# Column sums as adding transfers, and self entries of twelve columns, in a graph-and-experts kernel

## The reference

```
x   (1250, 512), src and dst (40000,): edges, dst sorted
xn  = layernorm(x)
h   = relu(xn @ W1 + b1) @ W2 + b2            # 512 -> 256 -> 512
agg[i] = sum of h[dst[e]] over edges e with src[e] == i
x1  = x + h + agg
xn2 = layernorm(x1)
gate = softmax(xn2 @ W_gate + b_gate); thr = sigmoid(xn2 @ W_thr + b_thr) * 0.25
w    = max(gate - thr, 0), divided by its sum over the 8 experts (1 where it is 0)
out  = x1 + sum over experts e of w[:, e] * (xn2 @ W_exp[e] + b_exp[e])
```

## Time and profile before

| | |
|---|---|
| median of 3 runs | 350.18 us (349.97 to 350.19) |
| the profiled execution | 349.31 us |
| its span, first to last instruction | 347.5 us |
| PE busy | 335.9 us, 97% of the span |
| DVE busy | 295.4 us, 85% |
| ACT busy | 119.4 us, 34% |
| POOL busy | 83.4 us, 24% |
| chain of waits, PE's share | 89%; DVE 5% |
| granted TensorE clock | 0.999 |
| bytes moved | 22.09 MB |

### The profile page before, as it was taken

The page is one execution under the profiler, slowest core; times in us unless marked ns, Lnnn a source line. Parts: engine busy times, 40 slices in busy tenths (PEclk is TensorE's granted clock), DMA queues, the critical chain, the costliest instruction groups (busy, mean ns, idle before and its releaser), DMA issues.

```text
span 347.5 us, 7647 instructions
## 1 busy us (share of the span) xinstructions
PE 335.9 (97%) x2637; PEld 261.4 (75%) x2637; DVE 295.4 (85%) x571; ACT 119.4 (34%) x233; POOL 83.4 (24%) x151
## 2 busy tenths in 40 slices
PE   8699999999999999999999999999999999999995
PEld 7589875665555645576678888888888888888884
DVE  7799999998896889977968888888898888888774
ACT  6898843454542036767213130030030200300000
POOL 5000032434343004429132140400500503200000
PEclk9999999999999999999999999999999999999999
DMA  7955132334443400040000030300300300000133
GB/s 171 253 155 195 49 85 52 80 75 96 88 86 86 136 0 0 2 126 3 0 0 2 6 116 3 116 7 2 123 1 2 121 2 2 1 2 0 61 119 120
DMA packets 20226, 22.09 MB, mean 64 GB/s; under 512 B 11850, under 2 KB 12647, under 8 KB 20188
## 3 DMA queue, kind: packets, MB, share of 16 engines
q1 hardware_dynamic: 17420, 18.36, 19.1%
q0 software_dynamic: 2352, 2.71, 3.4%
q10 hardware_dynamic: 416, 0.53, 0.7%
HBM read 12.77 MB, written 2.56 MB: 44 GB/s over the span
## 4 chain that ended last, share of the span: by engine, by line
PE 89%; DVE 5%; issue 2%; DMA 1%; ACT 1%; DVEq 0%; SPq 0%; ACTq 0%
PE ps_g L1195 13%; PE ps_g L1394 11%; PE ps_g L1396 11%; PE ps_g L1395 11%; PE ps_w L1255 8%; PE ps_g L1183 5%; PE ps_g L1318 3%; PE ps_a L1394 2%; PE ps_a L1396 2%; PE ps_a L1395 2%; PE ps_w L1394 2%; PE ps_w L1396 2%; PE ps_w L1395 2%; PE ps_w L1234 2%; PE ps_g L1360 2%
## 5 line engine op out<-in xcount | busy, mean ns | idle before, releaser
L1067 DVE SCALAR_TENSOR_TENSOR x_sb<-ps_g,weight_s,x_sb 125x256 f32<-125x256 f32 (+1 forms) x142 | 75.1, 547 | 19.5 <-PE ps_g L1396 18.4
L865 DVE TENSOR_TENSOR split<-places,keys 125x756 f16<-125x756 int16 (+4 forms) x119 | 73.2, 676 | 4.0 <-issue 2.2
L1394 PE MATMUL ps_g<-wb_hi,places 128*128 128x256 f16 x212 | 57.8, 273 | 0.1
L1396 PE MATMUL ps_g<-wb_hi,r_sb 128*128 128x256 f16 x212 | 57.8, 273 | 0.0
L1395 PE MATMUL ps_g<-wb_lo,places 128*128 128x256 f16 x212 | 57.8, 273 | 0.0
L1195 PE MATMUL ps_g<-late,r_sb 125*128 125x512 f32 (+3 forms) x120 | 51.5, 533 | 0.3 <-DMA late<-counts 0.2
L401 POOL DMA_DIRECT2D late<-counts x49 | 28.3, 577 | 79.6 <-ACT counts L599 79.0
L1255 PEld LDWEIGHTS ps_w<-split 125*128 125x128 f16 x476 | 29.9, 97 | 14.2 <-issue 6.4
L1396 PE MATMUL ps_g<-wb_hi,split 128*128 128x256 f16 x142 | 38.7, 273 | 0.0
L1394 PE MATMUL ps_g<-wb_hi,split 128*128 128x256 f16 x142 | 38.7, 273 | 0.0
L1395 PE MATMUL ps_g<-wb_lo,split 128*128 128x256 f16 x142 | 38.7, 273 | 0.0
(11 more groups left out here) (232 smaller groups left out, 675.3 us busy)
## 6 DMA issues: line engine op xcount, KB each, us to landing
stage<-in_L_ffn_W_exp_dram SPq DMA_DIRECT2D x8, 1024.0 KB, 5.2
late<-counts SPq DMA_DIRECT2D x54, 58.6 KB
late<-counts POOLq DMA_DIRECT2D x41, 58.6 KB, 2.8
x_sb<-in_x_dram SPq DMA_DIRECT2D x5, 448.0 KB, 11.5
out_dram<-x_sb SPq DMA_DIRECT2D x10, 224.0 KB
w_sb<-in_L_gnn_W_dram SPq DMA_DIRECT2D x2, 512.0 KB, 11.0
out_dram<-x_sb ACTq DMA_DIRECT2D x10, 26.0 KB
b_sb<-in_L_gnn_b_dram SPq DMA_DIRECT2D x1, 250.0 KB
```

The costliest lines, as they stand in the source:

```text
L865: nc.vector.tensor_tensor(hot[hot_at(stage, p)][:, 0:n, :].rearrange("p c (k x j) -> p c k x j", k=SEGS, j=2), places_of(windows[s], n), k ...
L1067: nc.vector.scalar_tensor_tensor(out=x_sb[:, i, a:z], in0=bank[0:R, at:at + z - a], scalar=weight_s[:, expert_of(u), i:i + 1], in1=x_sb[:, ...
L1394: nc.tensor.matmul(out_cols, hi_x, wb_hi[par][:, q, k, :], start=(opens and k == 0), stop=False, skip_group_check=True)
L1396: mm = nc.tensor.matmul(out_cols, lo_x, wb_hi[par][:, q, k, :], start=False, stop=(k == 1), skip_group_check=True)
```

## The change

Three edits.

1. **Column sums.** POOL issues a transfer for each of the tiles 0 to 8: tile 0 is copied to `a_sum`, tiles 1 to 8 are added to it by the transfer itself (`accum_op=ALU.add`), each 125 partitions of 1250 fp32, 625,000 bytes. A transfer waits for the tile's moves and for the sum before it. They stand behind POOL's move of group LAST[i] + 3 (SUM_LAG = 3; 9 for tile 0), and that of tile 8 behind the last group. Moves into a tile buffer wait for the transfer that read it. DVE keeps the last add alone (`last_sum`), behind the transfer of tile 8.
2. **Self entries.** One matmul for each run of rows that lies in one tile: its moving operand is 12 columns or fewer of `self_at` (the identity in fp16), its output the columns where the entries lie; all 128 partitions take part. Two matmuls in most groups, three in the nine border groups, one in the three groups with one window: 114 in place of 63. Two fills on POOL and one of two small ACT casts at the start fall away.
3. **Block sums.** Expert 1's four block sums on DVE move from behind groups 5, 6, 7, 8 to behind groups 28, 29, 31, 32.

```diff
-    SUM_LAG = 7
+    SUM_LAG = 3
...
-        self_lo = sb("self_lo", [128, 3 * LO + 2 * WIN], F16)
+        self_at = sb("self_at", [128, 2 * WIN], F16)
...
-                        eng.wait_ge(a_summed, max(tile - 3, 1))
+                        eng.wait_ge(a_added, 16 * (tile - 2))
...
+            def column_sum(i):
+
+                moved(pool, i)
+                if i > 0:
+                    pool.wait_ge(a_added, 16 * i)
+                if i == 0:
+                    pool.dma_start(a_sum, a_t[0]).then_inc(a_added, 16)
+                else:
+                    pool.dma_start(a_sum, a_t[i % 3], accum_op=ALU.add).then_inc(a_added, 16)
+
             begun = [2]
+            COLUMNS_AT = {max(LAST[i] + SUM_LAG, POOL_MOVES): i for i in range(TILES - 2)}
             for g in range(POOL_MOVES, NG):
                 pool.wait_ge(win_out, g + 1)
                 move(pool, g, 1, begun)
+                if g in COLUMNS_AT:
+                    column_sum(COLUMNS_AT[g])
+            column_sum(TILES - 2)
...
-            act.wait_ge(self_base, 2)
             act.wait_ge(const_ready, CONSTS)
-            for a in (0, WIN):
-                at = LO if a == 0 else 2 * LO + WIN
-                nc.scalar.activation(self_lo[0:2 * WIN, at:at + WIN], ident[0:2 * WIN, a:a + WIN], ACT.Copy).then_inc(self_ready, 1)
+            nc.scalar.activation(self_at[:, :], ident[:, 0:2 * WIN], ACT.Copy).then_inc(self_ready, 1)
...
-            def column_sum(i):
-
-                moved(dve, i)
-                if i > 1:
-                    dve.wait_ge(a_summed, i - 1)
-                nc.vector.tensor_tensor(a_sum, a_t[0] if i == 1 else a_sum, a_t[i % 3], ALU.add).then_inc(a_summed, 1)
+            def last_sum():
+
+                moved(dve, TILES - 1)
+                dve.wait_ge(a_added, 16 * (TILES - 1))
+                nc.vector.tensor_tensor(a_sum, a_sum, a_t[(TILES - 1) % 3], ALU.add).then_inc(a_summed, 1)
...
-            SUM_AT = {5: T1, 6: T3, 7: T2, 8: T4}
-            COLUMNS_AT = {LAST[i] + SUM_LAG: i for i in range(1, TILES - 2)}
+            SUM_AT = {28: T1, 29: T3, 31: T2, 32: T4}
...
-                if g in COLUMNS_AT:
-                    column_sum(COLUMNS_AT[g])
-            column_sum(TILES - 2)
...
-            column_sum(TILES - 1)
+            last_sum()
...
             def self_entries(g, pieces):
 
                 bank = ps_w[g % 2]
...
+                for n, (s, a, z, tile, at) in enumerate(MOVES[g]):
+                    own = nc.tensor.matmul(bank[:, s * LO + at:s * LO + at + z - a], self_pos[:, HI - 1 - tile:HI - 1 - tile + 128],
+                                           self_at[:, s * WIN + a:s * WIN + z], start=(n == 0), stop=False, skip_group_check=True)
+                    if n == 0 and g > 0 and g - 1 not in pieces and (g > SLOTTED or last_step_of(g - 1) % SLOT_STEPS > 0):
+                        own.then_inc(win_done, 1)
...
-            pe.wait_ge(a_summed, TILES - 1)
+            pe.wait_ge(a_summed, 1)
```

More of the change, by code:

```diff
@@ L130, in gnn_moe @@
         ones = sb("ones", [128, 128])
-        zeros = sb("zeros", [1, BANK], F16)
         eps = sb("eps", [128, 1])
@@ L270, in gnn_moe @@
         pool_moved = [sem(f"pool_moved{q}") for q in range(RINGS)]
-        a_summed = sem("a_summed")
+        a_summed, a_added = sem("a_summed"), sem("a_added")
         g_done = sem("g_done")
@@ L504, in _ @@
             group_rows(fill, (row_inv, "inv"), (row_size, "size"), (row_base, "base"))
-            nc.gpsimd.memset(zeros[:, :], 0.0).then_inc(self_ready, 1)
             nc.gpsimd.memset(self_pos[:, :], 0.0).then_inc(self_base, 1)
-            nc.gpsimd.memset(self_lo[:, :], 0.0).then_inc(self_base, 1)
-            pool.wait_ge(self_base, 2)
+            pool.wait_ge(self_base, 1)
             pool.wait_ge(const_ready, CONSTS)
@@ L1227, in self_entries @@
                 bank = ps_w[g % 2]
[L1228 to L1233, removed]
-                own = nc.tensor.matmul(bank[:, 0:cols], self_pos[0:rows, HI - 1 - tile:HI - 1 - tile + 128],
-                                       self_lo[0:rows, LO - at:LO - at + cols], start=True, stop=False, skip_group_check=True)
-                if g > 0 and g - 1 not in pieces and (g > SLOTTED or last_step_of(g - 1) % SLOT_STEPS > 0):
-                    own.then_inc(win_done, 1)
-                if not whole:
-                    a = 0 if rows <= WIN else LO
-                    nc.tensor.matmul(bank[:, a:cols], self_pos[:, HI - 2 - tile:HI - 2 - tile + 128],
-                                     self_lo[:, 2 * LO - at + a:2 * LO - at + cols], start=False, stop=False, skip_group_check=True)
+                for n, (s, a, z, tile, at) in enumerate(MOVES[g]):
[3 more added lines that the diff above has]
+                        own.then_inc(win_done, 1)
             def count(g, pieces):
@@ L1267, in count @@
                     one_step(stage, loop_of(g))
-            pe.wait_ge(self_ready, 4)
+            pe.wait_ge(self_ready, 2)
             pieces = {}
```

## The result

The changed kernel takes 389.44 us (median of 6 runs, 387.1 to 389.91), the one before 350.08 us (6 runs, 349.03 to 350.49): a ratio of 1.1125 with a 95% interval of 1.1101 to 1.1148, 39 us slower. The forecast was 352.1 us, its range ended at 356.5. The profiled execution took 388.63 us with a span of 386.8.

The account below looks back on a forecast made before the run. PE's own work was taken to bound the counting; -1.9 us from the self entries and +3.8 us of stall at its end make +1.9, so 349.31 becomes 351.2, plus 0.9 for the median 352.1 us; range 348.3 to 356.5.

Parts of the forecast that it names:

- What bounds the kernel: Counting stage: PE's own work sets the pace, 7.39 us a tile; DVE's 11.7 us of column sums are worth nothing there.
- The loop: Counting stage: one transfer per tile delays nobody if it takes less than 7.39 us.
- D: Time from issue to landing of tile 8's adding transfer, at the end of the counting: 7.2 us.
- all sixteen engines: Term of the last transfer's time: it runs on all DMA engines, not on five.
- The load's share: Term of the last transfer's time: expert 2's load, issued 0.6 us behind it, costs it 1.3 us.
- half of 398 GB/s: Rate of the adding transfer: two reads double a copy's 1.6 us for 0.625 MB to 3.1 us.
- The end: Ahead of the matmuls for `deg`: PE stalls for the last transfer's time less 3.4 us, 3.8 us on the path.
- The self entries: Self matmuls of the counting groups: narrow ones gain 2.1 us in nine border groups, less 0.2 us given back: -1.9 us.
- The floor of 0.055 us for a narrow matmul: Counting groups: a narrow self matmul is not shorter than 0.048 to 0.055 us, so ordinary groups stay at 0.11.
- PE's waits for its own issue: At the load of the step count behind the self entries: one more matmul ahead, 0.055 us four times, 0.2 us.
- The block sums: Expert 1's four sums, moved to groups 28 to 32: covered by DVE's lead, they gain and cost nothing.
- Five engines and two reads: Rival for the transfers: 13.0 us each, so sums and POOL's moves queue up, +39, 389 us; chance 0.05.

Follow-up runs that it names:

- `e4_no_sums`: The changed kernel with the column sums of tiles 0 to 8 left out altogether, narrow self entries and late block sums kept: 346.49 us, 0.9896 of the kernel before.
- `e8_rings`: The changed kernel with seven `counts` buffers in place of five: 389.51 us, 1.1134 of the kernel before.
- `e13_add_later`: The changed kernel with each add issued two groups later (SUM_LAG 5 in place of 3): 386.94 us, 1.1053 of the kernel before.
- `e2_plain_copy`: The changed kernel with plain copies of the same bytes in place of the adds: 362.55 us, 1.0363 of the kernel before.
- `e11_late_load`: The changed kernel with only tile 8's adding transfer, other sums on VectorE, and expert 2's load held until it landed: 354.91 us, 1.0153 of the kernel before.
- `e3_one_add`: The changed kernel with only tile 8's sum by an adding transfer, all others on VectorE: 356.28 us, 1.0182 of the kernel before.
- `e1_self_only`: The kernel before with the narrow self entries and nothing else: 347.47 us, 0.993 of the kernel before.

## Why the prediction was wrong, point by point

**What bounds the kernel: right.** PE bounds the counting, and VectorE's column sums are free; `e4_no_sums` confirms it.

**The loop: this step failed.** The prediction said that if the transfer takes less than 7.39 us "nobody waits: POOL's queue holds only moves there, with five `counts` buffers (seven us) of slack". The condition did not hold. In the loop, where no load of an expert is in the way, the prediction's own terms give D = 5.9 us; measured were 8.9. But 1.5 us above 7.39 on the seven adds of the loop are 11 us, and the counting lost some 32 (37.2 less the last stall of 5.2). The rest is the half that was never priced: what the transfer does to others. It takes every engine for six of its nine microseconds, so all moves, SP's as well, wait for its packets; GpSimd's land 7.7 us after their issue in the median from 52 to 150 us. The prediction charged contention only to the last transfer, by expert 2's load. Behind the landings stand three waits that can close a circle with the transfer: the moves of a tile have to be in before its add and its cuts (the changed kernel), a `counts` buffer has to be free (`e8_rings` removes it, nothing gained), a tile buffer has to be free (some tiles of `e13_add_later`). Shown are that the transfers cost 43 us, that the adding is the larger part, and that neither the `counts` buffers (0 us) nor the block's length (5) nor the place of the add (3) accounts for much of it; with a queue of their own they still cost 33. That the circles set the period is read from the waits and fits `e8_rings` and `e13_add_later`, but no run opened all three at once. Nor was the clock priced: behind 84 us it is down to 0.57 to 0.66 in several stretches of four microseconds, and the period grows from 11.6 to 12.6 us and more. No run filled PE's gaps in the loop, so what the clock costs there is not known.

**D: mis-sized.** Of the terms, all sixteen engines was right: 96.1% of them in the row above; five engines could not show more than 31%. The Trainium skill, DMA: Bandwidth & Descriptors, section "Why a DMA increments its semaphore by 16 and not by 1", leaves both open for 125 partitions (five by its rule, sixteen by its exception for some direct copies from GpSimd); the trace decides for sixteen. The load's share was forecast at 1.3 us and measured at 1.66. Wrong was the rate: half of 398 GB/s, 3.1 us, where the row shows 107 GB/s and 5.8 us. 398 GB/s was that of a load from HBM (395 packets of about 2000 bytes), and nothing on record tied it to transfers inside SBUF. A plain copy there does not reach it either: in `e2_plain_copy` all queues together moved 0.76 MB in the 3.6 us from 103.6 to 107.2 us, in the middle of a copy, or 211 GB/s.

**The end: form right, size not.** The stall of D - 3.4 us holds in four traces: 1.84 us at D = 5.39 (`e2_plain_copy`), 4.22 at 7.77 (`e11_late_load`), 5.23 at 8.83 (the changed kernel), 5.88 at 9.43 (`e3_one_add`). Unpriced was TensorE's clock: behind these stalls the stretch from `deg` to the last cuts, 4.70 us without one, took 2.5, 4.4, 4.6 and 4.8 us longer.

**The self entries: right sign, too small.** Forecast -1.9 us, measured -2.4 alone. The floor of 0.055 us for a narrow matmul was wrong: two take 0.04. That would be worth far more (0.07 us in 42 groups and 0.36 in nine, some 6 us), but part of it comes back: six counting matmuls take 0.35 us in the chain, before 0.33, about 1 us over all groups, and PE waits 1.4 us for DVE's comparisons in `e1_self_only`, before not at all. PE's waits for its own issue, which the prediction let grow by 0.2 us, went from 0.9 to 1.2. **The block sums: free**, as forecast, as far as 0.5 us with an interval from 1.2 off to 0.1 more can say.

**The rivals.** "Five engines and two reads" gave 389 us, the time that was measured, at a chance of 0.05. That it hit the number is luck. Its mechanism, sums that queue up and moves behind them, is near to what happened, but its 39 us are seven times 5.6, the excess of 13.0 over 7.39, and it has neither the stall at the end nor the clock. Measured were D = 8.9 us on all sixteen engines; by the same sum that would have been 11 us, and the rest came because the moves had no engines left.

## What to carry to other kernels

A transfer that is moved off a compute engine has to be priced twice: how long it takes from issue to landing, and how many engine-microseconds it takes from every other transfer that someone waits for; here small moves of 2.8 us became ones of 7, and the transfer's excess over the period explains only 11 of the 32 us that the counting lost. Before work is taken from an engine, leave it out altogether in one run: `e4_no_sums` shows that there was nothing to gain. Where PE will stall for some microseconds, count the stall about twice (1.8 us cost 2.5 more here, 5.9 cost 4.8 more), or fill it with matmuls that nobody needs.

## What the runs showed of the hardware

- An adding transfer from SBUF to SBUF of 125 x 5000 bytes ran at 107 GB/s on all sixteen engines and landed in 7.8 us alone, 8.9 in the loop and 9.4 beside a load; a plain copy of the same size landed in 5.3 us.
- After 5.9 us of stall the granted clock of the next ten microseconds was 0.50, with PE busy for 9.17 of them; with the stall filled it was 1.00. After 1.84 us of stall (`e2_plain_copy`) it was 0.66.
- Self entries of 12 columns and fewer stand 0.02 us apart in the chain (0.04 for two, 0.06 for three), less than half the distance of the counting matmuls of 125 columns (0.055).
- A matmul over a few rows (11 of 128) took 0.21 us in place of 0.11, and so did the one behind it. The weight loads of both began with their matmuls (88.69, 88.89); with 128 rows they began 0.38 and 0.11 us ahead of them.
- While an adding transfer had its packets of 5000 bytes on all sixteen engines (93.2 to 97 us), SP's queue, on which three moves were issued in that time, had no packet.
